# A hybrid RWKV, FP4 feed-forward and attention kernel: block maxima through a padded tile, and a new order of the steps in every tick

## The reference

```python
def fp4_quant_dequant(x):
    xb = x.reshape(shape[:-1] + (shape[-1] // BLOCK, BLOCK))          # BLOCK = 16
    scale = jnp.max(jnp.abs(xb), axis=-1, keepdims=True) / 6.0
    scale = jnp.maximum(scale, jnp.float32(1e-12))
    q = _GRID[jnp.searchsorted(_MID, jnp.abs(xb / scale))] * jnp.sign(xb) * scale
...
x = x + _L0_attn_a_ref(_layernorm(x), ...)       # 4 RWKV layers
x = x + _L0_ffn_ref(_layernorm(x), ...)          # down(silu(gate(x)) * up(x)), all fp4_linear, inner size 352
x = x + _L0_attn_b_ref(_layernorm(x), ...)       # causal attention
x = x + _L0_ffn_ref(_layernorm(x), ...)
```

## Time and profile before

| | us |
|---|---|
| median of 3 runs (1405.40 to 1406.56) | 1405.87 |
| the profiled execution, its own time | 1406.59 |
| its span from first to last instruction | 1405.2 |
| busy: PE / DVE / ACT / POOL | 1316.1 / 1269.7 / 1252.3 / 1161.1 |
| mean granted TensorE clock, as a share of full speed | 0.988 |

### The profile page before, as it was taken

How to read it: one execution, slowest core, us unless ns; L and a number is a source line. 1 busy time by engine, 2 the same in 40 slices (tenths; PEclk the granted TensorE clock), 3 DMA queues, 4 the chain that set the end, 5 groups by cost and what they waited for, 6 DMA issues and landing times.

```text
span 1405.2 us, 23693 instructions
## 1 busy us (share of the span) xinstructions
PE 1316.1 (94%) x7285; PEld 939.0 (67%) x7285; DVE 1269.7 (90%) x2169; ACT 1252.3 (89%) x2525; POOL 1161.1 (83%) x1218
## 2 busy tenths in 40 slices
PE   3689999999999999999999999989999999889996
PEld 1346666766666666666676776766767787666775
DVE  6999999999999999999999998669999666799994
ACT  6889999999999999999999998967778888868864
POOL 5888999999999999999997998979987533478874
PEclk9899999999999999999999999999999999999999
DMA  7000000001000000000000000100000000001011
GB/s 231 0 0 1 1 1 1 1 1 32 1 1 1 1 1 1 1 1 1 1 1 1 1 1 16 31 23 23 16 1 1 1 1 1 1 9 31 24 31 31
DMA packets 26925, 18.56 MB, mean 13 GB/s; under 512 B 1072, under 2 KB 26160, under 8 KB 26800
## 3 DMA queue, kind: packets, MB, share of 16 engines
q1 hardware_dynamic: 26800, 17.05, 4.1%
HBM read 12.85 MB, written 4.19 MB: 12 GB/s over the span
## 4 chain that ended last, share of the span: by engine, by line
PE 66%; DVE 20%; issue 7%; ACT 4%; POOL 2%; DMA 0%; DVEq 0%; SPq 0%; ACTq 0%; POOLq 0%
PE ps L1151 15%; PE ps L1134 13%; PE ps L1039 4%; PE ps L1141 4%; PE ps L1121 3%; PE ps L1104 3%; PE ps L1091 3%; PE ps L1092 3%; PE ps L1084 3%; DVE hsc L256 3%; PE ps L1260 2%; PE ps L1189 2%; PE ps L1242 2%; DVE W L463 2%; PE ps L1210 2%
## 5 line engine op out<-in xcount | busy, mean ns | idle before, releaser
L1151 PEld LDWEIGHTS ps<-W,kf 128*128 128x128 f32 x2048 | 246.8, 194 | 31.2 <-issue 30.1
L1134 PE MATMUL ps<-xk,W 128*128 128x512 f32 x512 | 262.6, 595 | 1.4 <-DVE W L463 1.4
L1151 PE MATMUL ps<-W,kf 128*128 128x128 f32 x2048 | 252.2, 277 | 0.0
L756 ACT ACTIVATE z<-X,ln_rs 128x128 f32<-128x128 f32 x512 | 233.9, 674 | 3.2 <-POOL ln_rs L605 3.1
L866 ACT ACTIVATE kf<-ps 128x512 f32<-128x512 f32 x256 | 197.5, 771 | 1.9 <-PE ps L1134 1.7
L873 ACT ACTIVATE kf<-kf 128x1024 f32<-128x1024 f32 x128 | 158.9, 1242 | 0.0
L1039 PEld LDWEIGHTS ps<-idn,z 128*128 128x128 f32 x664 | 81.8, 144 | 98.9 <-issue 61.5
L1039 PE MATMUL ps<-idn,z 128*128 128x128 f32 x664 | 103.7, 280 | 42.6 <-DVE aa L366 20.5
L712 POOL TENSOR_TENSOR W<-W,hsc 128x704 f32<-128x704 f32 x64 | 88.7, 1386 | 46.2 <-DVE W L493 46.2
L1134 PEld LDWEIGHTS ps<-xk,W 128*128 128x128 f32 x512 | 87.0, 192 | 58.7 <-issue 56.4
L603 POOL TENSOR_TENSOR ln_rs<-ln_rs,mhalf 128x8 f32<-128x8 f32 (+1 forms) x70 | 124.0, 1771 | 0.0
(11 more groups left out here) (178 smaller groups left out, 3986.0 us busy)
## 6 DMA issues: line engine op xcount, KB each, us to landing
X<-x_in SPq DMA_DIRECT2D x16, 256.0 KB, 6.6
xi<-x_in SPq DMA_DIRECT2D x16, 256.0 KB, 2.9
out<-X SPq DMA_DIRECT2D x16, 256.0 KB, 2.3
W<-weights SPq DMA_DIRECT2D x4, 832.0 KB, 8.5
W<-fp4w SPq DMA_DIRECT2D x1, 560.0 KB, 3.7
row<-rows SPq DMA_DIRECT2D x1, 192.0 KB, 2.9
wqkv<-qkv SPq DMA_DIRECT2D x1, 96.0 KB, 5.8
idn<-ident SPq DMA_DIRECT2D x1, 64.0 KB, 3.2
```

The source lines that it names most:

```text
L756: last = e.activation(chunk(dst, j), chunk(src, j), ACT.Identity, bias=rs[:, 1, j:j + 1], scale=rs[:, 0, j:j + 1])
L1134: e.matmul((pF0, pF1)[f % 2][:, :], w_of(r, WCK + f), xk[r % 2][:, :], start=True, stop=True).then_inc(kf_mm[f], 1)
L1151: last = e.matmul(chunk(pKV, j), kf[r % 3][:, f, j * 128:(j + 1) * 128], w_of(r, WCV + f), start=f == 0 and j == 0, stop=f == 3, skip_grou ...
```

## The change

The change has two parts.

First, the block maxima of the hidden tensor. Before, `fh_max` wrote 88 maxima side by side into one half of tile hsc, and `fh_scale` read them there. Now the input is viewed as 11 groups of 8 blocks of 16, and the maxima go into a new tile `ham` of 11 rows of 9 numbers, of which 8 are used; `fh_scale` reads that padded view and writes 88 numbers side by side into hsc as before. The wait for the reader of the old hsc contents moves from `fh_max` to `fh_inverse`. The input's own `fx_scale` is unchanged.

Second, the lists of steps of DVE, POOL, ACT and PE are written in a new order, some steps with another lag: `gate` and `ff_values` one tick earlier, `ff_gate` and `tanh_c` two, `add_xb` one; `f_z`, `fx_divided`, `rsqrts`, `sub_dh`, `add_num`, `mix_rt`, `arg_r` and `args` stand one tick later in number (several of them move from the end of a tick to the head of the next); `put_x`, `keep_hq(.., 0)` and `h_turn(.., 1)` move from the head of a tick to the end of the one before. FFN_AT becomes NR + 3, so the whole program has 133 ticks.

```diff
-Q_AT = 55
-FFN_AT = NR + 4
+Q_AT = 56
+FFN_AT = NR + 3
 LN2_LAG = 6
 EARLY = 10
-GAP = NB
+GAP = 16
...
-        hsc = ring("hsc", 2, [128, 2, 88])
+        hsc, ham = ring("hsc", 2, [128, 2, 88]), ring("ham", 2, [128, 11, 9])
...
             def block_max(am, values):
-                return e.tensor_reduce(am, blocks(values), AX, ALU.max, apply_absolute_value=True)
+                return e.tensor_reduce(am, values, AX, ALU.max, apply_absolute_value=True)
...
-                    block_max(xsc[n % 2][:, 0, :], fz[n % 3]).then_inc(fx_am, 1)
+                    block_max(xsc[n % 2][:, 0, :], blocks(fz[n % 3])).then_inc(fx_am, 1)
...
             def fh_max(n):
                 if n in range(2 * NB):
                     w.wait_ge(hu_done, NT * n + NT)
-                    w.wait_ge(fh_y[1], n - 1)
-                    block_max(hsc[n % 2][:, 0, :], hh[n % 3]).then_inc(fh_am, 1)
+                    w.wait_ge(fh_s, n - 1)
+                    block_max(ham[n % 2][:, :, 0:8], hh[n % 3].rearrange("p (a k b) -> p a k b", a=11, b=16)).then_inc(fh_am, 1)
...
-                    block_scale(hsc[n % 2][:, 1, :], hsc[n % 2][:, 0, :]).then_inc(fh_s, 1)
+                    block_scale(hsc[n % 2][:, 1, :].rearrange("p (a k) -> p a k", a=11), ham[n % 2][:, :, 0:8]).then_inc(fh_s, 1)
...
             def fh_inverse(n):
                 if n in range(2 * NB):
+                    w.wait_ge(fh_y[1], n - 1)
                     w.wait_ge(fh_s, n + 1)
...
-                weights_rounded(t - Q_AT - 6)
...
+                weights_rounded(t - Q_AT - 4)
...
-                turn2(t - 9)
-                ff_values(t - 13, 1)
...
+                turn2(t - 9)
```

More of the change, by code:

```diff
@@ L532, in vector @@
             for t in range(TICKS):
+                mix_rt(t - 5)
+                arg_r(t - 6)
+                a_mask(att_job(t - 7), 3)
                 mix_t(t - 5)
                 fh_add(ffn_job(t - 8), 0)
-                fx_max(ffn_job(t - 3))
[L536 to L541, removed]
@@ L557, in vector @@
-                fx_inverse(ffn_job(t - 3))
+                fh_sub(ffn_job(t - 8), 0)
+                mul_up(ffn_job(t - 7), 3)
+                fh_max(ffn_job(t - 7))
+                weights_rounded(t - Q_AT - 4)
+                init_affine(t - 2)
+                mix_r(t - 11)
+                gated(t - 7)
+                a_max(att_job(t - 7), 3)
+                a_inverse(att_job(t - 8))
+                fh_add(ffn_job(t - 8), 1)
+                mix_k(t - 10)
+                mul_rv(t - 6)
@@ L558, in vector @@
+                fh_scale(ffn_job(t - 7))
+                scan_bb(t - 6)
+                fh_sub(ffn_job(t - 8), 1)
+                mul_s1(t - 6)
+                weights_scales(t - Q_AT)
+                fx_max(ffn_job(t - 3))
                 fh_inverse(ffn_job(t - 7))
                 a_add(att_job(t - 8))
-                bn2(t - 8)
+                add_xa(t - 8)
+                mul_up(ffn_job(t - 6), 0)
                 fx_add(ffn_job(t - 4))
-                weights_scales(t - Q_AT)
-                mul_up(ffn_job(t - 6), 0)
+                fx_scale(ffn_job(t - 3))
@@ L564, in vector @@
+                scan_aa(t - 6)
+                fx_sub(ffn_job(t - 4))
                 a_mask(att_job(t - 6), 0)
+                scan_pp(t - 5)
                 a_max(att_job(t - 6), 0)
-                fx_sub(ffn_job(t - 4))
-                scan_pp(t - 5)
                 bn1(t - 2)
@@ L570, in vector @@
                 sub_d(t - 5)
+                fx_inverse(ffn_job(t - 3))
+                bn2(t - 8)
                 a_mask(att_job(t - 6), 1)
+                prepare(t - 3)
+                a_max(att_job(t - 6), 1)
                 mul_u(t - 7)
+                a_mask(att_job(t - 6), 2)
                 init_stats(t)
-                gate(t - 13)
+                a_max(att_job(t - 6), 2)
+                gate(t - 12)
                 mul_up(ffn_job(t - 6), 2)
+                f_bn(ffn_job(t))
                 rwkv(t - 7)
[L577 to L582, removed]
                 a_bn(att_job(t))
@@ L985, in scalar @@
             for t in range(TICKS):
-                keep_hq(ffn_job(t - 9), 0)
                 silu(ffn_job(t - 7), 3)
-                put_x(ffn_job(t - 9))
+                weights_out(t - Q_AT - 14)
+                keep_hq(ffn_job(t - 9), 1)
                 keep_hq(ffn_job(t - 9), 2)
+                fh_magic(ffn_job(t - 8), 1)
+                args(t - 6)
+                f_z(ffn_job(t - 3))
+                keep_h1(t - 4)
+                keep_ax(att_job(t - 5))
+                keep_fx(ffn_job(t - 5))
@@ L1031, in scalar @@
                 seeds(t - 6)
+                relu(t - 11, 3)
+                keep_hq(ffn_job(t - 8), 0)
         def tensor():
@@ L1273, in tensor @@
-                turn1(t - 4)
-                values(t - 6)
-                lend_M(ffn_job(t - 8), 1)
+                f_turn(ffn_job(t - 5))
+                lend_T(t - 6)
+                f_gate(ffn_job(t - 6), 0)
+                p_values(att_job(t - 8))
+                down(ffn_job(t - 9))
+                receptance(t - 6)
                 ff_keys(t - 11, 1)
                 output(t - 8)
-                lend_T(t - 6)
-                f_turn(ffn_job(t - 5))
-                ff_keys(t - 11, 2)
@@ L1305, in tensor @@
-                p_turn(att_job(t - 7), 3)
-                weights_in(t - Q_AT - 14)
-                lend_M(ffn_job(t - 7), 0)
-                h_turn(ffn_job(t - 8), 0)
+                similarity(att_job(t - 6), 0)
+                keys(t - 5)
+                lend_O(t - 7)
+                p_turn(att_job(t - 7), 1)
+                ff_values(t - 12, 0)
+                f_up(ffn_job(t - 6), 1)
+                ff_keys(t - 11, 2)
+                ff_values(t - 12, 1)
+                similarity(att_job(t - 6), 1)
```

129 lines of the change are left out of this document (52 added, 77 removed).

## The result

The change makes the kernel slower: 1411.09 us (median of 13 runs, 1409.95 to 1412.14) against 1405.87 (13 runs, 1403.85 to 1411.24). The ratio is 1.0033, 95% interval [1.0021, 1.0045]; the quotient of the two medians is 1.0037. Of all 86 executions of the kernel before on record 19 took 1408.8 to 1411.5 us, about as long as the changed kernel, and the 15 of these whose clock is listed had a mean granted clock of 0.987 or 0.988, where most others had 0.99. The profiled execution took 1410.86 us, its span 1409.3 against 1405.2 before. The forecast was 1401.7 and "faster".

The account below looks back on a forecast made before the run. Bounds taken: ACT and PE in RWKV, POOL in the first FFN, PE in attention, DVE in the second FFN. From 1406.59, 2.8 - 2.0 - 3.5 - 1.5 = -4.2 gives 1402.4, median-adjusted 1401.7; range 1389 to 1413.

Parts of the forecast that it names:

- The hsc scale is freed: FFN, DVE's scale on 88 numbers: no longer waits for POOL's wide operation, saving 0.36 us a tick.
- The xsc scale in the second FFN: Scale on 32 numbers is held by POOL's L706: +0.64 us a tick; with the hsc saving, ten ticks give +2.8.
- Ticks with `add_res` stay at POOL's 10.5: 0: First FFN ticks with `add_res`: POOL is full, so the tick stays at 10.5 us, change 0.
- rival B: First FFN: POOL's `fx_scaled` waits for `fx_sub` behind the held scale; +4.9 us over seven ticks, 1413.6 total, chance 0.18.
- RWKV ticks: RWKV part: work per tick unchanged and ACT full, so 0; bounds 0 and 1.0 us a tick.
- The weights: FFN weights' rounding on DVE: PE's idle in front of `turn2` gets cover, -2.0 us, bounds 0 and -4.
- The removed tick: Overlap of RWKV and first FFN: one tick less gives back half of PE's idle, -3.5 us, bounds -7 and +3.
- The end: Last ticks: PE's waits for `keep_hq` before `down` shrink by earlier steps, -1.5 us of 4.3, bounds 0 and -4.3.
- Attention into the second FFN: Overlap from 1217 to 1255 us: new order, no gain tied to it, 0, bounds -5 and +4.

Follow-up runs that it names:

- the first two that split pairs: On the kernel with the scale behind `fx_sub`: `mul_up(.,3)` between `fh_add` and `fh_sub`, 1402.47 us; or `f_bn` there and `mul_up(.,0)` behind `fx_add`, 1400.97 us.

## Why the prediction was wrong, step by step

- **The hsc scale is freed.** Right: 231 to 245 ns everywhere, and from start to start it takes 0.32 us less in the second FFN's tick (0.36 predicted).
- **The xsc scale in the second FFN.** Right in place and nearly in size: it starts 0.67 us into L707 and the tick loses 0.56 (0.64 predicted). The tick was to be 10.54 and is 10.73. The missing 0.2 is a term that I left out: the new order puts two dependent pairs back to back. I added up durations where I should have read, for each new neighbourhood, whether the second operation needs the first. Over ten ticks that is up to +1.9; the two stretches below have 1.4 of it.
- **"Ticks with `add_res` stay at POOL's 10.5: 0."** This is the step that failed. I argued that POOL is full and so DVE's lateness costs nothing. But POOL waits for the late instruction itself. The tick is 11.26, six of them cost 4.5 us (B: 0.7 to 0.8 a tick, seven ticks, +4.9), and the one-line move of `fx_scale` takes all of it back. The mechanism was written down as rival B, with its price; what put it at 0.18 was the remark that POOL "drifts to where the scale is held by L712 instead". The trace shows no drift: in all six ticks the scale takes 1.28 to 1.30 us, and POOL waits 0.71. The run with the scale ahead shows how near the escape was: 0.6 us earlier, and the tick is 10.64.
- **RWKV ticks.** Right, 13.20, and the trace bears out the reason, that ACT is full. `rwkv` (L387) now comes up beside POOL's L673 and takes 1.37 us instead of 0.91, and DVE has no idle time left in the tick. But L673 has itself waited 0.92 us for ACT, and POOL waits for nothing behind it in the tick, so this hold closes no circle. Behind a long tick `rwkv` takes 0.68 and DVE gets its 21 operations done in 12.5 us; ACT, busy all the time in both, then ends fewer of its own (25, not 27), so it cannot keep that up. That is read from the trace; no run moves `rwkv`. DVE and then POOL in the tick of 13.20, then a tick of 12.50 (columns as in rows 2):

```profile
605.05 1.37 DVE L387 SCALAR_TENSOR_TENSOR rc<-er,p 128x512 f32<-128x512 f32 x1
```

```profile
604.83 1.04 POOL L673 TENSOR_TENSOR dh<-h 128x512 f32<-128x512 f32 x1 [0.92 <-ACT h L860]
```

```profile
708.90:721.40 12.50, 12.50 (x69) 8.62 (x68) 12.50 (x21) 12.50 (x25) 12.24 (x12) 1.00 0.00 1
```

- **The weights.** Wrong: -2.0 predicted, nothing gained. The two traces differ by +0.6, which is within what this stretch varies: at a granted clock of 1.00 it took 200.3 us both in the order of before (the run with the padded tile alone) and in the new one (the run with the tick put back). PE still idles, for 2.20 us (row below). I took PE's idle for the cost; the cost is DVE's four operations in a tick in which DVE has no room, which makes it 17.3 us. The cover I counted on lay on PE, which was not short of work.

```profile
751.35 1.11 PE L1040 MATMUL ps<-idn,z 128*128 128x128 f32 x4 [2.20 <-DVE aa L366]
```

- **The removed tick.** Right in sign, -3.5 predicted, -2.6 between the two traces and some -4 by the run that puts it back.
- **The end.** -0.8 of -1.5. The granted clock there was 0.91 before and 0.82 after; in three runs of the new order with 0.99 (the first two that split pairs, and the moved rounding) the end took 18.1 to 18.2 us, against 19.1 in the run with 8 rows of 12, which has the old order and 1.00. So at the same clock the gain is about 1.0. The waits for `keep_hq` are 1.68 and 1.58 instead of 2.80 and 1.50:

```profile
1395.70 4.83 PE L1211 MATMUL ps<-WD,W 128*128 128x128 f32 x24 [1.68 <-ACT W L929]
1403.42 2.92 PE L1211 MATMUL ps<-WD,ed 128*128 128x128 f32 x24 [1.58 <-ACT ed L929]
```

- **Attention into the second FFN.** 0 predicted, -1.9 in the trace. Some 1.3 of it go with the clock: it was 0.86 there before and 0.92 after, and the run with the scale behind `fx_sub`, in the new order at 0.85, took 23.2 us, against the 23.8 before and the 21.9 after. No run isolates the rest.

Summed over the table's stretches, measured less predicted: +5.0 in the ticks with `add_res`; +0.2, +1.2 and +0.7 in the other FFN ticks (+0.8, +3.4 and +0.7 where 0.6, 2.2 and 0 were counted); +2.6 for the weights; +0.9 for the removed tick; +0.7 at the end; -1.9 where attention runs out, +0.1 in attention and -1.3 in the first 650 us. That is 8.2, against 8.3 between the spans' +4.1 and the forecast's -4.2. More than half of it, 4.5, is the one circle in the first FFN. The -1.3 is within the spread: to `scan_pp` of job 48 the runs of the new order took from 653.5 to 656.1 us.

## What to carry to other kernels

When an operation that can be held by another engine is moved, look at what stands behind it on its own engine, and whether the engine that holds it waits for that: a hold that closes into a circle costs even an engine that is full. When adding up a new order, give each operation that directly follows its producer its extra time (0.12 us here), and check each step pulled forward against the end of its operand's producer. Idle time of one engine behind another's one-off work is no saving if the other engine is full in that tick. And before a difference between two traces is put down to the order, compare the granted clock of that stretch in both.
